# Direct sums of 40 of 125 columns per chunk, with float32r products and the message in the weights

## The reference

```python
def _L2_gnn_ref(x, edge_index, W1, b1, W2, b2):          # sheaf
    ...
    msg_s = coef[:, None] * jnp.einsum('eij,ej->ei', L_sd, xd)
    msg_d = coef[:, None] * jnp.einsum('eji,ej->ei', L_sd, xs)
    out = x - jnp.zeros_like(x).at[src].add(msg_s) - jnp.zeros_like(x).at[dst].add(msg_d)
    ...
def _L3_gnn_ref(...):                                    # product
    m = jnp.einsum('ei,ej,ijh->eh', x_j, edge_attr_e3nn, W_msg_tp) * norm_msg_tp
    m = jax.nn.silu(m)
    m = m @ W_msg_lin * norm_lin
    agg = jax.ops.segment_sum(m, row, num_segments=n_nodes)
```

## Time and profile before

| what | value |
|---|---|
| time, median of 3 runs | 39062.36 us (39044.63 to 39074.47) |
| the profiled execution's own time | 39271.15 us |
| its span | 39269.4 us |
| PE, PEld busy | 14491.4, 10823.7 us (37%, 28%) |
| DVE busy | 16153.8 us (41%) |
| ACT busy | 2598.4 us (7%) |
| POOL busy | 22323.1 us (57%) |
| mean granted clock of TensorE | 0.624 |

### The profile page before, as it was taken

The page is one execution under the profiler, slowest core; times in us unless marked ns, Lnnn a source line. Parts: engine busy times, 40 slices in busy tenths (PEclk is TensorE's granted clock), DMA queues, the critical chain, the costliest instruction groups (busy, mean ns, idle before and its releaser), DMA issues. The chain is left out here.

```text
span 39269.4 us, 263864 instructions
## 1 busy us (share of the span) xinstructions
PE 14491.4 (37%) x71326; PEld 10823.7 (28%) x71326; DVE 16153.8 (41%) x34514; ACT 2598.4 (7%) x3901; POOL 22323.1 (57%) x20450
## 2 busy tenths in 40 slices
PE   1111110111111056664666433344334334066664
PEld 1100000110101045554555322222222222044443
DVE  2332247232323556774666523233233333344443
...
GB/s 44 14 12 12 11 11 117 21 21 19 21 19 22 113 23 27 29 29 17 28 29 30 20 9 12 9 9 11 10 9 9 9 11 8 54 14 13 15 15 47
DMA packets 1089161, 934.54 MB, mean 24 GB/s; under 512 B 580668, under 2 KB 1031892, under 8 KB 1063892
## 3 DMA queue, kind: packets, MB, share of 16 engines
...
## 5 line engine op out<-in xcount | busy, mean ns | idle before, releaser
L1124 POOL DMA_INDIRECT messages<-se_M,se_rstage x2625 | 2977.0, 1134 | 3850.5 <-DVE se_M L1487 3057.4
L1124 POOL DMA_INDIRECT messages<-pe_M,pe_rstage x2625 | 3132.6, 1193 | 1094.3 <-issue 792.6
L493 POOL DMA_INDIRECT g1g_G<-tab,g1g_stage x3125 | 3036.9, 972 | 1038.4 <-issue 1027.6
L493 POOL DMA_INDIRECT se_G<-tab,se_stage x3125 | 3027.7, 969 | 1039.5 <-issue 1025.0
L493 POOL DMA_INDIRECT g2g_G<-tab,g2g_stage x3125 | 2961.8, 948 | 1038.5 <-issue 1020.2
L1432 DVE TENSOR_TENSOR se_V<-se_pTV,s_b 128x160 f32 (+1 forms) x625 | 203.0, 325 | 6605.0 <-remote 4158.7
L493 POOL DMA_INDIRECT c2c_G<-tab16b,c2c_stage x2125 | 2482.7, 1168 | 659.1 <-issue 641.8
L493 POOL DMA_INDIRECT c1c_G<-tab,c1c_stage x2125 | 2480.7, 1167 | 659.1 <-issue 641.0
L1023 DVE SCALAR_TENSOR_TENSOR g2gh_junk<-g2gh_pB,g2gh_src_f,earlier 128x128 f32<-128x128 f32 (+4 forms) x2625 | 1458.0, 614 | 2726.0 <-remote 1811.4
L724 PE MATMUL g1gh_acc<-g1gh_oh_hi,g1gh_oh_lo 128*128 128x100 bf16 x6250 | 780.5, 272 | 4614.0 <-issue 3650.8
L1521 PE MATMUL se_pTV<-ident,se_pair 128*32 128x128 f32 x3125 | 599.8, 339 | 4715.0 <-DVE se_pair L1428 2428.1
...
## 6 DMA issues: line engine op xcount, KB each, us to landing
...
g1g_G<-tab,g1g_stage POOLq DMA_INDIRECT x3125
g2g_G<-tab,g2g_stage POOLq DMA_INDIRECT x3125
```

Of the source, the lines that this page charges most:

```text
L493: g.indirect_dma_start(out=G[b][:, t, :], out_offset=None, in_=table, in_offset=bass.IndirectOffsetOnAxis(ap=stage[b][:, t:t + 1], axis=0) ...
L1124: g.indirect_dma_start(out=view, in_=M[b][:, DC + t, :], in_offset=None, out_offset=bass.IndirectOffsetOnAxis(ap=stage[b][:, t:t + 1], axis=0)
```

## The change

`DG` goes from 4 to 8, so that 40 columns of each chunk are direct and 85 scattered; the sides count 17 groups a chunk (9 and 8 in the convolutions). The sum of one column is made in another way: the node number is split into a slot of 8 (`MR`) and a row out of 13 x 128 = 1664. DVE compares a row of counters (float16) with the column's row number (1664 elements, float32r out) and multiplies the message, which `prepare` has split into two float32r parts for the chunk, with the one-hot of its slot (256 elements). PE takes these 256 as weights of 128 in each of two parts, over the 1664 in four banks: eight float32r matmuls over 416. `tensor_last` turns the sum back with 13 transposes at the stage's end. In the sheaf stage a step now makes two columns on DVE and adds the same two on PE, in a loop of 5 rounds with 4 steps written out, and 3 plain steps written out. In the product stage 9 plain groups come first and then 16 steps with 2, 3, 2 and 3 columns. Some buffers change their scope.

```diff
-DG = 4
+DG = 8
...
     def products(self, pe, b, start):
-        for q in range(self.BANKS):
-            mm = pe.matmul(self.acc[:, q, 0:self.w * D], self.oh_lo[b][:, :],
-                           self.wide[b][:, q * self.w:(q + 1) * self.w, :].rearrange("p t d -> p (t d)"),
-                           start=start, stop=True, skip_group_check=True)
+        for n in range(PARTS):
+            for q in range(self.BANKS):
+                mm = pe.matmul(self.acc[:, q, 0:self.w], self.spot[b][:, n, :, :].rearrange("p r f -> p (r f)"),
+                               self.hot[b][:, q * self.w:(q + 1) * self.w],
+                               start=start and n == 0, stop=True, skip_group_check=True)
...
+    def prepare(self, v, ch, M, i):
...
+        ch(v.tensor_copy(self.part[:, :, 0, :], values))
+        ch(v.tensor_tensor(self.part[:, :, 1, :], values, self.part[:, :, 0, :], ALU.subtract))
+        ch(v.tensor_scalar(self.slot_i[:, :], k.src_i[:, at], 7, MR - 1, ALU.logical_shift_right, ALU.bitwise_and))
+        ch(v.tensor_copy(self.slot[:, :], self.slot_i[:, :]))
+        ch(v.tensor_tensor(self.slot_hot[:, :, :], bc(self.slot[:, :], [P, DC, MR], 2),
+                           bc(k.iota[:, 0:MR], [P, DC, MR], 1), ALU.is_equal))
+        ch(v.tensor_tensor(self.row[:, :], k.src_hi[:, at], self.slot[:, :], ALU.subtract))
+        ch(v.tensor_scalar(self.row[:, :], self.row[:, :], float(P // MR), None, ALU.mult))
+        ch(v.tensor_tensor(self.row[:, :], self.row[:, :], k.src_lo[:, at], ALU.add))
...
-        v.tensor_tensor(self.oh_lo[b][:, :], k.iota[:, :], k.src_lo[:, at].to_broadcast([P, P]),
+        v.tensor_scalar(self.hot[b][:, :], self.count[:, :], self.row[:, at], None,
                         ALU.is_equal).then_inc(self.made, 1)
-        v.tensor_tensor(self.oh_hi[b][:, :], k.iota[:, 0:NT], k.src_hi[:, at].to_broadcast([P, NT]),
-                        ALU.is_equal).then_inc(self.hot, 1)
-        v.wait_ge(self.hot, m + 5)
-        v.tensor_tensor(self.wide[b][:, :, :], bc(self.oh_hi[b][:, :], [P, NT, D], 2),
-                        M[:, bass.ds(d, 1), 0:D].to_broadcast([P, NT, D]), ALU.mult).then_inc(self.made, 1)
+        shape = [P, PARTS, MR, D]
+        v.tensor_tensor(self.spot[b][:, :, :, :],
+                        self.slot_hot[:, at, :].unsqueeze(3).to_broadcast(shape),
+                        self.part[:, at, :, :].rearrange("p a n f -> p (a n) f").unsqueeze(2).to_broadcast(shape),
+                        ALU.mult).then_inc(self.made, 1)
...
+    def tensor_last(self, pe):
+        pe.wait_ge(self.moved, self.BANKS)
+        for j in range(MJ):
+            mm = pe.transpose(self.acc[:, j // 4, (j % 4) * P:(j % 4 + 1) * P], self.total[:, j * P:(j + 1) * P],
+                              self.k.ident[:, :])
+        mm.then_inc(self.turned, 1)
...
+ROUNDS, STEPS, PER_STEP = 5, 4, (2, 2, 2, 2)
+LATE_ROUNDS, LATE_STEPS, PER_LATE = 4, 4, (2, 3, 2, 3)
...
-                    spread_column(0, 0)
                     evacuate(0)
-                    with v.Fori(0, DC // 2 - 1) as m:
-                        ch.enter(m, 10)
-                        group_step(2 * m + 1, 1)
-                        group_step(2 * m + 2, 0)
-                        ch.leave(DC // 2 - 1, 10)
-                    group_step(DC - 1, 1)
-                    with v.Fori(DC, NG - 1) as q:
-                        ch.enter(q - DC, 5)
+                    with v.Fori(0, ROUNDS) as m:
+                        ch.enter(m, 5 * STEPS)
+                        for n in range(STEPS):
+                            group_step(STEPS * m + (n + 1), direct_columns(m, n) if direct_before else ())
+                        ch.leave(ROUNDS, 5 * STEPS)
+                    for q in range(ROUNDS * STEPS + 1, NG - 1):
                         group_step(q)
...
+                    if direct_before:
+                        v.wait_ge(sums.made, i * (2 * DC))
+                    sums.prepare(v, ch, M[b], i)
...
-                    with pe.Fori(0, DC // 2) as m:
-                        for half in range(2):
-                            group_step(2 * m + (1 + half), 2 * m + half if direct_before else None, half)
-                    with pe.Fori(DC + 1, NG - 1) as q:
+                    with pe.Fori(0, ROUNDS) as m:
+                        for n in range(STEPS):
+                            group_step(STEPS * m + (n + 1), direct_columns(m, n) if direct_before else ())
+                    for q in range(ROUNDS * STEPS + 1, NG - 1):
                         group_step(q)
...
-                    with v.Fori(0, DC // 2) as m:
-                        outer_products(2 * m + (DG + 1))
-                        sums.vector(v, k, M[b], i, 2 * m, 0)
-                        outer_products(2 * m + (DG + 2))
-                        sums.vector(v, k, M[b], i, 2 * m + 1, 1)
+                    v.wait_ge(sums.made, i * (2 * DC))
+                    sums.prepare(v, ch, M[b], i)
+                    v.nop(nofuse=True)
+                    with v.Fori(0, LATE_ROUNDS) as m:
+                        for n in range(LATE_STEPS):
+                            outer_products(LATE_STEPS * m + (DG + 1 + n))
+                            for d, half in direct_columns(m, n, PER_LATE):
+                                sums.vector(v, i, d, half)
...
-                    with pe.Fori(0, DC // 2) as m:
-                        for half in range(2):
-                            n = i * NG + 2 * m + (DG + 1 + half)
+                    with pe.Fori(0, LATE_ROUNDS) as m:
+                        for step in range(LATE_STEPS):
+                            n = i * NG + LATE_STEPS * m + (DG + 1 + step)
                             transpose(n)
-                            sums.tensor(pe, i, 2 * m + half, half)
+                            for d, half in direct_columns(m, step, PER_LATE):
+                                sums.tensor(pe, i, d, half)
                             multiply(n)
```

143 lines of the change are left out of this document (83 added, 60 removed).

## The result

The changed kernel takes 39572.94 us (median of 4 runs, 39381.38 to 39658.13) beside 39053.49 us (4 runs, 38825.88 to 39074.47): 1.0123 of the time before, 95% interval 1.0076 to 1.0171. It is slower, where the forecast had it 230 us faster. It is within the range, and rival (a) is the case that came, by its second condition: no chunk stays fast.

A forecast was written before the change was run, and what follows sets the result against it. POOL was taken to bound the product, a chain over DVE, PE and ACT the sheaf stage; -315 - 400 - 33 - 260 + 750 = -258, rounded to -230, gave 38830 us, range 37600 to 39650 (8 in 10).

The forecast's parts named there:

- rival (a): Sheaf stage: dense steps at 12.1 us or no chunk stays fast; +209 to +1190, middle +400, 39460 us; chance 0.27.
- the break-even interval of 470 us: Sheaf stage: the interval between messages at which its loss eats the 1008 us gained elsewhere.
- The likeliest case: Whole kernel: sheaf cost of 400 to 1000 us with the other gains kept, 38500 to 39050; chance 0.42.
- I take +750: Sheaf stage: loss of 750 us chosen between +517 (six fast chunks kept) and +1217 to +1464 (none).
- Per slow chunk -29 + 58 + 3 = +32: Sheaf stage: 20 fewer scatters save 29 us, steps behind POOL cost 58 more, `prepare` 3; +32 us a slow chunk.
- the price of the step: Sheaf steps with two columns behind POOL's transfers: 8.5 us at full clock, 12.1 at 1.2 GHz, mix about 9.5.
- (b): Sheaf stage: float32r columns keep PE at 2.4 GHz and the stall away; 35800 to 38050 us; chance 0.14.
- the low price of 4.0 us a group: Convolutions: one side group fewer saves 4.0 us a chunk, -400 us in all; the whole-stage price 7.6 gave -760.
- the stall's 1.4 us an instruction: Sheaf stage: while POOL issues transfers and PE is at the low clock, each PE instruction costs 1.4 us.
- less what the 20 scatters took out of the stall, up to 30: Product: a deduction from 187 us a chunk, leaving 157 to 187; 159 taken, about -260 us.
- (c): Product gains nothing, its engines the new bound; 0 to +100 us in place of -260, 39090 to 39190; chance 0.08.
- (d): New longer loop bodies: each back-branch costs 3.66 us, 220 branches, 805 us, 39635 us in all; chance 0.05.

The follow-up runs named there:

- e0b_after: The changed kernel unaltered, run again on the fourth chip, where PE does not stall: 31720.14 us, ratio 0.9718 to the kernel before.
- e1b_ahead: The changed kernel with DVE making sheaf columns one ahead of PE, on the fourth chip, where PE does not stall: ratio 0.9694 to the kernel before.
- e1_ahead: The changed kernel with DVE making sheaf columns one ahead of PE: on the stalling second chip 39010.29 us beside 39681.44 for the kernel before, ratio 0.9842.
- e3_late: The changed kernel with the sheaf's columns only in its last 16 steps, stalling second chip: 40548.07 us, ratio 1.0230 to the kernel before.

## Why the prediction was wrong

**The sign.** The sum had -1008 outside the sheaf stage, +750 in it. It came out as -907 and +1272 (the sheaf stage without its scans), in one profiled execution, and the break-even interval of 470 us was right: 481.6 is above it. The likeliest case was chosen wrongly, by its sheaf term.

**The step that failed.** It is "I take +750", a value between +517 (six chunks stay fast) and +1217 to +1464 (none does). None stayed fast, and the measured +1272 lies in the range that the prediction itself gave for that case. By the table of intervals, the short ones that went cost 624 of the 1281 us. The prediction gives no reason for any of them to stay; what it names beside the number (serial waits leave PE gaps, the fast chunks had PE at 1.0) speaks for the high value. Why the short intervals went is not shown: they come and go with the chip in the kernel before too (five and one), and none of the runs with other orders and forms on stalling chips has one.

**The step that held.** "Per slow chunk -29 + 58 + 3 = +32" came out as +36 on the chip of the result. POOL's part of a slow chunk, from its messages to POOL's last transfer, went from 315.9 to 290.4 us (-26), and what is behind it from 137.7 to 198.8 (+61; means of the 18 and the 23). In those 17.6 steps were left before (I had 18) and 19.0 after (I had 19.7), and the steps with columns take 10.2 us, where I had 9.5. The fifth chip is less kind: -26 + 73 = +47, with 21.2 steps left after.

**What sets the 10.2 us.** I had named the serial wait and had put it into the price of the step, at 8.5 at the full clock and 12.1 at the low one. What I did not see is that the order of DVE and PE sets the clock too: e0b_after and e1b_ahead, on one chip, differ in nothing but the order and have 0.77 and 1.00, in 102 and 70 us. With one column ahead a stalling chip gives 0.984 and not a loss. That much of the cause is shown: with the columns made ahead, the 40 direct columns pay.

**Slips in the working.** The sum is -258 and would be 38800; "rounded, -230" and 38830 don't follow, which changes neither sign nor range. In (b), a third of the chunks slow would be 8 x 61 - 16 x 93 = -1000 in the stage, 37050, and not 37400. The last interval was counted among the fast chunks.

**What else was right.** On this chip: the attention layer (-320 for -315), the convolutions (-427 for -400; the low price of 4.0 us a group, not the 7.6 of the whole stages), the scans, DVE's price of a column (1.50 for 1.65, its bounds 1.6 to 2.0 a little high: the compare is 1.084 us for 1.21 to 1.56), the stall's 1.4 us an instruction, and the product's steps (7.4 or 7.7 and 3.8 in turn, 5.6 to 5.75, for 5.6).

**The product.** -143 with its scans for -276. Its steps were right, but POOL's wait for its messages grew by 537 us, and with the dearer scatter (1.55 for 1.495) that took most of the 747 that the 20 scatters are worth. Nine plain groups, two of them still stalled (9 and 20 us in the trace), come before the steps. The term that was mis-sized is "less what the 20 scatters took out of the stall, up to 30", of which I took 28; with the other terms as they were, chunks of 4100 / 25 = 164 us say 23.

**The rivals.** (a) is what happened, through no fast chunk; the dense steps were at 10.2 and not at 12.1. (b), float32r products that keep PE at 2.4 GHz and the stall away, was wrong: the clock in the dense steps fell from 0.94 to 0.77, and e1_ahead, with 1.00 in its dense steps, has its stalled steps all the same. (c) did not come on this chip in full, and came at 60 columns. (d): the round's back-branch shows no gap of 3 us, the steps of a round take 9.8, 9.9, 10.6 and 10.7 us. The rule of the Trainium skill, page "Runtime: NRT & Kernel Launch", section "Instruction fetch mechanics", did not bear on these bodies: no gap of that kind stands at a round's end in the trace.

**A better kernel.** e1_ahead, the changed kernel with one column made ahead, beats both: 0.984 of the kernel before where PE stalls, 0.964 to 0.969 where it doesn't. Beside the changed kernel on one chip it is 83 us faster where PE is free (fourth chip); where PE stalls, the two stand at 0.984 and 1.009 to 1.012, each against the kernel before on its own chip.

**What stays open.** What makes PE pay 1.4 us an instruction on some chips; why the kernel before has five short intervals on one such chip and one on another, and no later kernel has any; why e1_ahead's interval is 448 and not 432; and how e1_ahead and the changed kernel stand on one stalling chip (the nearest pair on one is e1_ahead and e3_late, 39010 and 40548 us, and e3_late has its columns in other steps too).
